# One more causal product on VectorE, one fewer on GpSimd, and a new order of the first phase

## The reference, cut to what matters

```
h = layernorm(x) * (1 + ca) + sa
x = x + ga * linear_attention(h)         # first half, "phase A" of the kernel
h = layernorm(x) * (1 + cb) + sb
x = x + gb * two_layer_local_attention_ffn(h)   # second half, "phase L", two layers
```

## Time and profile before

| what | value |
|---|---|
| median of three runs | 3249.38 us (3248.24 to 3250.14) |
| profiled execution, its own time | 3245.92 us |
| its span, first to last instruction | 3244.1 us |
| busy: PE, DVE, ACT, POOL | 97%, 82%, 66%, 79% of the span |
| mean granted TensorE clock | 0.991 |
| phase A, first projection to last instruction of POOL | 37.8 to 600.5 us |

### The profile page before, as it was taken

One profiled execution on the slowest core, in us unless ns is written; L12 is line 12 of the kernel. 1 busy time (PEld: TensorE's weight loads), 2 busy tenths in 40 slices (PEclk: granted clock), 3 DMA queues, 4 the chain that ended last, 5 costly groups with the idle time before them and its releaser, 6 DMA issues.

```text
span 3244.1 us, 85014 instructions
## 1 busy us (share of the span) xinstructions
PE 3139.3 (97%) x25436; PEld 2434.1 (75%) x25436; DVE 2654.7 (82%) x8312; ACT 2146.4 (66%) x5372; POOL 2575.4 (79%) x2892
## 2 busy tenths in 40 slices
PE   5999999699999999999999999999999999999998
PEld 3677677467777777777777777777777777777777
DVE  5899999578777777777777788888888888888885
ACT  3656666367767676767676777776767676767674
POOL 3999999687777777777777778888888888888885
PEclk8999999899999999999999999999999999999999
DMA  6211111000000000000000001111111111111111
GB/s 217 80 46 48 49 46 47 29 21 24 24 25 24 25 24 25 24 25 24 25 24 25 24 25 37 37 37 38 37 38 37 38 37 38 37 38 37 38 37 30
DMA packets 153077, 125.03 MB, mean 39 GB/s; under 512 B 22580, under 2 KB 149032, under 8 KB 152368
## 3 DMA queue, kind: packets, MB, share of 16 engines
q1 hardware_dynamic: 146352, 110.67, 11.2%
q10 hardware_dynamic: 6272, 8.93, 0.9%
HBM read 77.51 MB, written 42.02 MB: 37 GB/s over the span
## 4 chain that ended last, share of the span: by engine, by line
PE 91%; POOL 3%; issue 2%; DVE 2%; ACT 1%; DMA 1%; ACTq 0%; SPq 0%; DVEq 0%; POOLq 0%
PE bank L541 33%; PE bank L737 19%; PE bank L745 10%; PE bank L548 9%; PE bank L710 7%; PE bank L689 6%; PE bank L604 2%; PE bank L622 2%; POOL shared L1269 1%; PE bank L584 1%; PE bank L587 1%; PE bank L633 1%; PE bank L615 1%; DMA X<-in_x 0%; PE bank L723 0%
## 5 line engine op out<-in xcount | busy, mean ns | idle before, releaser
L737 PEld LDWEIGHTS bank<-zT,W 128*128 128x128 f32 x5632 | 667.1, 192 | 137.2 <-issue 134.8
L1305 POOL TENSOR_TENSOR rnorm<-clamped,HALF 128x8 f32<-128x8 f32 x256 | 420.5, 1643 | 413.7 <-DVE clamped L1135 407.2
L541 PE MATMUL bank<-WQKV,xT 128*128 128x512 f32 x1536 | 743.5, 607 | 5.3 <-DVE rotary_work L1118 4.4
L737 PE MATMUL bank<-zT,W 128*128 128x128 f32 x5632 | 671.0, 275 | 13.7 <-issue 11.7
L1318 POOL TENSOR_TENSOR shared<-shared,share_of 128x512 f32<-128x512 f32 x512 | 585.3, 1171 | 59.3 <-DVE shared L1170 59.3
L906 ACT ACTIVATE shared<-shared,negmax 128x256 f32<-128x256 f32 x1024 | 505.6, 495 | 27.2 <-DVE negmax L1154 25.7
L541 PEld LDWEIGHTS bank<-WQKV,xT 128*128 128x128 f32 x1536 | 263.8, 192 | 216.1 <-issue 214.0
L1132 DVE TENSOR_REDUCE sums<-rotary_work 128x8 f32<-128x512 f32 x256 | 175.5, 685 | 287.5 <-ACT rotary_work L876 283.7
L1170 DVE COPY_PREDICATED shared<-BEYOND,shared 128x256 f32<-128x256 int32 x512 | 400.0, 793 | 0.0
L1154 DVE CUSTOM_DVE_ANT_0 shared<-bank,MASK 128x256 f32<-128x256 f32 x1024 | 365.8, 420 | 0.1
L1328 POOL TENSOR_TENSOR shared<-shared,IDENT 128x256 f32<-128x256 f32 x512 | 362.4, 729 | 0.0
(11 more groups left out here) (153 smaller groups left out, 6638.3 us busy)
## 6 DMA issues: line engine op xcount, KB each, us to landing
X<-xl_rows SPq DMA_DIRECT2D x128, 128.0 KB, 2.2
X<-in_x SPq DMA_DIRECT2D x64, 128.0 KB, 2.1
x_tiles<-ax SPq DMA_DIRECT2D x64, 128.0 KB, 1.7
xl_rows<-axl SPq DMA_DIRECT2D x64, 128.0 KB, 1.7
XS<-xl_rows SPq DMA_DIRECT2D x128, 64.0 KB, 2.1
xm_rows<-X SPq DMA_DIRECT2D x128, 64.0 KB, 1.6
xs<-xm_rows SPq DMA_DIRECT2D x128, 64.0 KB, 1.8
xl_rows<-X SPq DMA_DIRECT2D x64, 128.0 KB, 1.7
```

The lines of the kernel that those rows point to most:

```text
L541: mm = nc.tensor.matmul(held(tile, key)[:, 0:cols], lhsT[c], rhs[c], start=(c == 0), stop=(c == len(lhsT) - 1))
L737: mm = nc.tensor.matmul(held(tile, key)[:, k * P:(k + 1) * P], W1[:, tile.l, c, at:at + P], zT[:, c], start=(c == 0), stop=(c == KC - 1))
L1305: G.tensor_tensor(rnorm[q][:], clamped[q][:], HALF[:].to_broadcast((P, LH)), ALU.pow).then_inc(done[f"root_{key}"], 1)
```

## The change

The three tables of phase A are replaced, and the table of banks of phase L. One causal product (`a_mask1`) moves from ACT plus POOL to DVE, and `a_copy1` goes away. No other step is added or removed, and no step function is edited. In the new DVE order `a_mask1` stands last in its slot with delay 3, `a_mask2` and `a_mask3` first in the next with delay 4.

```diff
-COPIED = 2
+COPIED = 1
 ORDER_A = {
-    "SP": [(0, "a_modulation"), (0, "a_load"), (5, "a_keep_x1"), (6, "a_store")],
-    "PE": [(2, "a_project_v"), (3, "a_sum"), (4, "a_number"), (1, "a_turn_z"), (2, "a_cum"), (3, "a_score"), (1, "a_project"),
-           (4, "a_out"), (2, "a_turn_q")],
-    "ACT": [(2, "a_exp"), (3, "a_keep_q"), (4, "a_keep_o"), (1, "a_affine"), (2, "a_keep_kphi"), (2, "a_keep_cum"),
-           (3, "a_copy0"), (3, "a_copy1")],
-    "DVE": [(5, "a_gate"), (6, "a_norm2"), (2, "a_phi"), (5, "a_stats2"), (2, "a_value"), (0, "a_stats"), (3, "a_state"),
-           (2, "a_prod"), (0, "a_norm"), (2, "a_queries"), (3, "a_mask2"), (1, "a_bias"), (3, "a_mask3")],
-    "POOL": [(5, "a_x1"), (6, "a_mod"), (5, "a_root2"), (0, "a_root"), (4, "a_add_state"), (0, "a_pre"), (3, "a_mask0"),
-           (3, "a_mask1")],
+    "SP": [(0, "a_modulation"), (0, "a_load"), (6, "a_store"), (5, "a_keep_x1")],
+    "PE": [(1, "a_project"), (2, "a_cum"), (4, "a_number"), (1, "a_project_v"), (4, "a_out"), (0, "a_turn_z"), (3, "a_score"),
+           (2, "a_sum"), (2, "a_turn_q")],
+    "ACT": [(3, "a_keep_q"), (1, "a_exp"), (2, "a_keep_kphi"), (4, "a_keep_o"), (2, "a_keep_cum"), (0, "a_affine"),
+           (3, "a_copy0")],
+    "DVE": [(4, "a_mask2"), (4, "a_mask3"), (2, "a_value"), (3, "a_state"), (1, "a_bias"), (5, "a_stats2"), (0, "a_stats"),
+           (2, "a_prod"), (5, "a_norm2"), (0, "a_norm"), (1, "a_phi"), (2, "a_queries"), (4, "a_gate"), (3, "a_mask1")],
+    "POOL": [(4, "a_mask0"), (5, "a_x1"), (5, "a_root2"), (0, "a_root"), (4, "a_add_state"), (0, "a_pre"), (5, "a_mod")],
 }
...
 BANK_A = {
-    "av": "27475705", "kv": "01010161", "num": "52642746", "az": "33333333", "kphi": "52642540", "cum": "74757652",
+    "num": "12310523", "av": "64756471", "awo": "47562316", "az": "31647564", "sc1": "52312407", "sc2": "16475523",
...
 BANK_L = {
-    "qT": "21530626", "k": "74747474", "nw": "30606215", "z": "62151530", "sim0": "15306212", "sim1": "74747474",
-    "sim2": "21530626", "sim3": "30621535", "o": "62153430", "v": "74747475", "ag2": "62171530", "kT": "06215306",
+    "z": "70707070", "sim3": "70707070", "sim2": "54316252", "sim1": "31625434", "sim0": "16254313", "o": "25431616",
+    "v": "54316254", "ag2": "70757070", "kT": "62543162", "q": "31625433", "ag0": "25474316", "ag1": "16262543",
...
-              "sc0": "a_copy", "sc1": "a_copy", "sc2": "a_mask", "sc3": "a_mask", "num": "a_keep_o", "kv": "a_state",
+              "sc0": "a_copy", "sc1": "a_mask", "sc2": "a_mask", "sc3": "a_mask", "num": "a_keep_o", "kv": "a_state",
```

More of the change, by code:

```diff
@@ L81 @@
 BANK_A = {
-    "av": "27475705", "kv": "01010161", "num": "52642746", "az": "33333333", "kphi": "52642540", "cum": "74757652",
-    "sc0": "10101616", "sc1": "52642740", "sc2": "74757052", "sc3": "65264274", "aqk": "33333333", "awo": "10151610",
-    "aq": "52642640",
+    "num": "12310523", "av": "64756471", "awo": "47562316", "az": "31647564", "sc1": "52312407", "sc2": "16475523",
+    "sc3": "00001640", "sc0": "31230752", "kv": "52312307", "aq": "64756431", "aqk": "23164756", "cum": "52312357",
+    "kphi": "00000024",
 }
 BANK_L = {
[4 rows of a table removed]
[3 rows of a table added]
 }
```

## The result

The changed kernel takes 3269.93 us (median; 3269.5 to 3273.28) beside 3248.81 us (3245.75 to 3250.14) for the kernel before in the same measurement: a ratio of 1.0071, 95% interval 1.0058 to 1.0084. It is slower by 21 us, 0.7%. The forecast was 3260 us, range 3241 to 3271: the direction and the engine that becomes the bound are as forecast, the loss is twice the one worked out, and most of what the sum lacks lies in phase L.

What follows compares the result with a forecast made beforehand. PE bounds both phases before; DVE was to bound phase A after. Steady +8, loop ends +3, rotary 0, filling -3, draining +4, phase L 0: 3249.4 + 11 to 12 = 3260 us, range 3241 to 3271.

Steps and rivals of the forecast that it cites:

- DVE as the bound: Phase A: DVE's slot becomes 8.47 us, over PE's 8.29, so DVE sets the pace; chance 0.43.
- the lock waits: DVE in phase A: `a_phi` runs alone, 1.10 to 0.68 us; L1058 is held behind POOL's product, +0.35.
- The steady term: Phase A's steady slots: +0.18 us in about 50 slots, +9; a slot-by-slot count gave +7; taken as +8.
- Loop ends: Phase A: DVE's slack no longer swallows its stops at four loop ends, 4 x 0.67 = +3 us, bounds 0 and +4.
- Rotary products: Products behind `a_mod` in mid phase A, five left there of six: 0 us, bounds -4 and +2.
- Filling: Start of phase A, where DVE waits for the eighth tile's load: -3 us, bounds -4 and +1.
- Draining: End of phase A: rounds of about 6.4 us, 30 us for 25.8, so +4 us, bounds -2 and +6.
- Phase L: Phase L with its new bank table: same set of waits, same length, 0 us.
- a different length would mean that a bank is waited for: Sign for phase L: a changed length means a bank there is waited for, putting the sum beside the point.
- DVE hidden: Rival in phase A: L1058 isn't held, DVE's slot is 8.12, under 8.29; 3250 us, no change; chance 0.29.
- a shorter PE slot: Rival in phase A: one tile-shape switch on PE goes away, 56 x 0.15 = 8 us; 3242 us; chance 0.18.
- The much slower rival: Rival in phase A: no relief on DVE, slot 8.68 and more, `a_phi` still at 1.1; 3273 us; chance 0.10.

Runs made afterwards that it cites:

- e1: Changed kernel with `a_gate` ahead of `a_queries` in DVE's list: 3258.43 us, ratio 1.0040 to the kernel before.
- e3: Changed kernel with phase L's bank table of the kernel before, phase A untouched: 3267.96 us, ratio 1.0065 to the kernel before.
- e4: Kernel before with phase L's new bank table alone: 3247.40 us, ratio 1.0003 to the kernel before.
- e9: Kernel before with 63 instructions of long-satisfied waits added on DVE between the phases: 3249.93 us, ratio 1.0011 to the kernel before.
- e12: e1 with one more long-satisfied wait instruction on DVE between the phases: 3256.34 us, ratio 1.0030 to the kernel before.
- e8: Changed kernel with two products on ACT plus POOL again and `a_gate` ahead of `a_queries`: 3302.24 us, ratio 1.0171 to the kernel before.
- e2: Changed kernel with `a_queries` ahead of `a_norm2` and `a_norm` in DVE's list: 3286.20 us, ratio 1.0120 to the kernel before.
- e10: Changed kernel with PE's `a_out` behind `a_score` and DVE's `a_gate` last, behind `a_mask1`: 3289.73 us, ratio 1.0135 to the kernel before.
- e11: Changed kernel with PE's `a_score` ahead of `a_turn_z`, `a_out` behind it, and DVE's `a_mask1` ahead of `a_queries`: 3299.47 us, ratio 1.0163 to the kernel before.

## Where the prediction was right, and where it failed

Of the 11.6 us by which the sum for the span fell short, 7.2 are phase L, put at nothing, 3.4 the 56 slots and 1.7 the drain; filling and the start together gave 0.7 back.

- **DVE as the bound, the lock waits, their order in time**: right, each of them, and e1 shows it by an experiment. `a_phi` 0.68 (forecast 0.68), L1056 0.88 (forecast 0.77, in its bounds). By its own row of before it would have stayed at 0.42. The Trainium skill ("SBUF — State Buffer", section "Who interferes with whom") says that a VectorE instruction with two SBUF inputs contends with a GpSimd one that reads SBUF, and that the one that issues second blocks: the trace agrees, in both directions (L1056 second: 0.88; POOL second: 0.95 for 0.79 in e1).
- **The steady term, mis-sized**: +8 forecast, 56 x 0.226 = +12.7 measured. Two steps failed. The straight sum gave a slot of 8.47 and +9, and I took +8 for a slot-by-slot count of 8.42 in which other waits looked better; `a_norm` did fall, from 804 to 728 ns median, but L1056 cost 0.11 more than put in, and the slot is 8.52. And I counted 50 slots: those with a rotary product or a loop's end carry the longer DVE slot too, so it is all 56.
- **Loop ends** +3: about +3.1 in the slots around the four ends. The sum is right, its sign is not quite: the slots at the ends are 1.95 to 2.15 over the others, not 2.3 to 2.5, and the slot ahead of each carries another 0.4. e1 shows a limit of the reason: with DVE 0.19 under PE's slot the slots at the ends still take 10.5 to 10.7, so this little slack swallows nothing.
- **Rotary products** 0: -1.9, in the bounds. **Filling** -3: -4.2, just past its bound, and +0.5 ahead of it.
- **Draining** +4: +5.7, in the bounds. The round of 6.4 us was right (6.44); the end came out 1.5 us later than the 30 us that it gave. That belongs to the new order (27.66 with the product alone, 38.36 with the order alone).
- **Phase L** 0: +7.2, the step that failed most. "The set of waits is the same" was right for the banks (e3, e4), and so the sign "a different length would mean that a bank is waited for" was wrong. The sum went from "no bank waits" to "same length" and left out two things. Phase A's code has another length, so DVE's phase L began 63 instructions later: that is the seven late tiles, 1.4 us (e9 and e12 show it). And PE's granted clock, taken as 1.00, was 0.50 in two of PE's last groups: 3.3 us, which e4 and e8 show without DVE's displacement, e4 without the new phase A too. The last 2.5 us are not settled.
- **The rivals.** DVE hidden was 3250 and a shorter PE slot 3242; e1, with DVE relieved, gives PE's list 8.34, longer by 0.05. So even without the lock wait of L1056 the change would not have been faster. The much slower rival needed `a_phi` at 1.1; it took 0.68.

The range held the result by 1 us, and by luck: it had no bound for phase L, and took the loss there only because the bounds of the drain and of L1058 were wide.

## What to carry to other kernels

When an engine has 0.2 us to spare in a slot, cost the lock waits as well as the work: list which two-input DVE instructions would be in flight with a POOL product in the new order, and who starts first. Look for a step without a second SBUF input to put into the gap (the gate, in e1: 8.52 to 8.34), but only where no one waits for what it pushes back (e2, e10, e11). And a stage that an edit doesn't touch can still change by a few microseconds, as its code moves (1.4 us here) or PE's clock falls in it (3.3): measure its length on its own, and allow for it in the range.

## What the runs showed of the hardware

- One instruction more or less ahead of a loop shifts a stall of 0.36 us on DVE to or from the same instruction in one tile of eight (e1: 0.75, e12: 0.40 idle ahead of L1184; e9: 0.75). The trace names the last semaphore, not the stall. The Trainium skill ("Runtime: NRT & Kernel Launch", section "Instruction fetch mechanics") says that engines take their instructions in blocks of 256 and that a branch out of the blocks at hand stalls. The stops of 2.3 to 2.5 us at loop ends fit this; a stall that comes and goes with one instruction is not in it, and no run here shows its cause.
- The lock works both ways, and 0.2 us of start time decide: L1056 0.13 us behind POOL's start takes 0.88; 0.07 us ahead of it, 0.43, and POOL's product 0.95.
- Taking DVE's lock waits away made the kernel slower (e2, +0.5%), since the order that did it brought `z` to PE later.
- With the same waits of PE ahead, the end of phase L ran at a granted clock of 1.00 in the kernel before and at 0.50 in two groups of matmuls of the changed one, which took 4.05 and 3.95 us for 2.40. No run here shows what decides it.
